# Expert stage of a routed feed-forward layer: which engine reads the expert weights from where

## The reference, cut to what matters

```python
x = x + xattn(layernorm(x), ctx, ctx, mask, ...)
# feed-forward, on layernorm(x); E = 8 experts, D = 128, F = 512
gates = max(softmax(xt @ Wr + br)); idx = argmax(...)
xn = layernorm(xt) * ln_g + ln_b
h = relu(xn @ W1[idx] + b1[idx])        # W1[e] is 128 x 512
y = h @ W2[idx] + b2[idx]               # W2[e] is 512 x 128
x = x + y * gates
```

## Time and profile before

| what | value |
|---|---|
| median of three runs | 397.69 us |
| the profiled execution | 394.74 us |
| its span on the core | 393.0 us |
| VectorE busy | 304.9 us (78%) |
| TensorE matmul busy | 303.1 us (77%) |
| ScalarE busy | 202.0 us (51%) |
| expert stage, first `xh` to last `ot` | 285.7 to 384.7 us |

### The profile page before, as it was taken

How to read it: one execution, slowest core, us unless ns; L and a number is a source line. 1 busy time by engine, 2 the same in 40 slices (tenths; PEclk the granted TensorE clock), 3 DMA queues, 4 the chain that set the end, 5 groups by cost and what they waited for, 6 DMA issues and landing times.

```text
span 393.0 us, 10023 instructions
## 1 busy us (share of the span) xinstructions
PE 303.1 (77%) x3066; PEld 240.2 (61%) x3066; DVE 304.9 (78%) x1159; ACT 202.0 (51%) x548; POOL 163.5 (42%) x220
## 2 busy tenths in 40 slices
PE   0449888788998878877798988963079898978990
PEld 0327656556875655654585776762078887867880
DVE  1247899999989999999999999756747776767771
ACT  1127666466456555646546465511056666656650
POOL 3314445455435545545544543333104443434442
PEclk9999989978568997999968595555569999999997
DMA  5955543234325333424324324000011112112110
GB/s 127 416 132 145 147 137 104 84 111 136 87 85 155 93 90 107 136 84 139 110 85 133 89 84 125 10 14 14 16 42 43 54 54 61 42 50 64 54 32 3
DMA packets 58228, 36.31 MB, mean 92 GB/s; under 512 B 5295, under 2 KB 56116, under 8 KB 58176
## 3 DMA queue, kind: packets, MB, share of 16 engines
q1 hardware_dynamic: 54592, 31.30, 27.5%
q0 software_dynamic: 2272, 4.27, 3.3%
q10 hardware_dynamic: 1312, 0.11, 0.5%
HBM read 14.03 MB, written 22.09 MB: 92 GB/s over the span
## 4 chain that ended last, share of the span: by engine, by line
issue 37%; DVE 31%; POOL 15%; DMA 6%; PE 5%; DVEq 2%; ACTq 1%; POOLq 1%; SPq 0%; ACT 0%
POOL rows_dram L355 5%; DVE Pr L539 3%; DVE mx L535 3%; POOL rs L333 3%; POOL row L343 3%; DMA out<-ot,G 3%; DVE hT L660 3%; DVE xt L500 3%; DVE xh L648 3%; DVE ot L669 2%; POOL xb L338 2%; POOL Kb L348 2%; DMA G<-rows_dram 2%; DVE yb L667 2%; DMA Wr<-in_wr 1%
## 5 line engine op out<-in xcount | busy, mean ns | idle before, releaser
L366 POOL DMA_INDIRECT out<-ot,G x39 | 39.8, 1020 | 67.8 <-DVE ot L669 66.7
L343 POOL TENSOR_TENSOR row<-ve,half 128x2 f32<-128x2 f32 x32 | 24.7, 771 | 103.1 <-DVE ve L589 103.1
L413 ACT ACTIVATE Pr<-Pr,rowany 128x1024 f32<-128x1024 f32 x32 | 36.7, 1148 | 59.8 <-DVE Pr L539 59.8
L706 PE MATMUL ps<-ident,Pr 128*128 128x128 f32 x256 | 51.2, 335 | 0.1
L396 ACT ACTIVATE PT<-ps 128x512 f32<-128x512 f32 x64 | 38.2, 597 | 18.4 <-PE ps L706 17.6
L706 PEld LDWEIGHTS ps<-ident,Pr 128*128 128x128 f32 x256 | 37.0, 173 | 16.8 <-issue 9.1
L796 PE MATMUL ps<-xg,WR 128*128 128x128 f32 x312 | 45.5, 291 | 0.0
L752 PE MATMUL ps<-VB,PT 128*64 128x18 f32 x1024 | 42.1, 228 | 0.3 <-ACT GT L403 0.3
L535 DVE TENSOR_REDUCE mx<-ps 128x16 f32<-128x1024 f32 x32 | 38.9, 1216 | 3.3 <-PE ps L695 3.3
L807 PE MATMUL ps<-WR,hT 128*128 128x128 f32 x312 | 41.2, 276 | 0.0
L796 PEld LDWEIGHTS ps<-xg,WR 128*128 128x128 f32 x312 | 39.5, 199 | 1.4
(11 more groups left out here) (113 smaller groups left out, 633.8 us busy)
## 6 DMA issues: line engine op xcount, KB each, us to landing
rows_dram<-empty SPq DMA_DIRECT2D x32, 528.0 KB, 4.4
WA<-in_wpk SPq DMA_DIRECT2D x8, 578.0 KB, 9.2
G<-rows_dram SPq DMA_DIRECT2D x39, 66.0 KB, 1.9
X<-in_x SPq DMA_DIRECT2D x32, 64.0 KB, 4.1
C<-in_ctxT SPq DMA_DIRECT2D x32, 64.0 KB, 1.8
Cv<-in_ctxT SPq DMA_DIRECT2D x32, 64.0 KB, 2.0
out<-ot,G POOLq DMA_INDIRECT x39, 2.3
rows_dram<-row,posi POOLq DMA_INDIRECT x32, 2.5
```

The lines of the kernel that those rows point to most:

```text
L366: g.indirect_dma_start(out=out, out_offset=bass.IndirectOffsetOnAxis(ap=G[:, q, D + 2:D + 3].bitcast(I32), axis=0), in_=ot[:, q, :], in_of ...
L413: a.activation(Pr[:, q, :], Pr[:, q, :], ACT.Exp, scale=rowany[:, 0:1]).then_inc(s_p, 1)
L706: last = nc.tensor.transpose(ps[:, 4 + m, 128 * j:128 * j + 128], Pr[:, q, 128 * (4 * m + j):128 * (4 * m + j) + 128], ident[:])
```

## The change

The tile `WA` is laid out in another order per expert: W1, b1, b2 and then W2. The ring `WR` holds only W1, b1 and b2 (644 values a partition instead of 1156). ScalarE copies all three of them in one instruction, and VectorE copies nothing. TensorE loads the slot's expert number from `slot` into a register and reads W2 in the down projection straight from `WA` at an address made from it. As the ring buffer now also holds the biases, ScalarE's copy waits for two more readers of the old contents.

```diff
-WP = F + FC * D + FC + D
+WS = F + FC + D
+WP = WS + FC * D
...
-        WR = sb("WR", [P, NW, WP])
+        WR = sb("WR", [P, NW, WS])
...
-        def w2_of(s, c):
-            return WR[:, s % NW, F + D * c:F + D * c + D]
+        def w2_of(ex, c):
+            return WA[:, bass.ds(ex, 1), WS + D * c:WS + D * c + D].rearrange("p e d -> p (e d)")
...
 # ScalarE, stage_w1(s)
                 ex = act.value_load(slot[0:1, 0, s:s + 1], min_val=0, max_val=E - 1)
                 wait(act, b_up, s - NW + 1)
-                a.activation(WR[:, s % NW:s % NW + 1, 0:F], WA[:, bass.ds(ex, 1), 0:F], ACT.Copy).then_inc(b_w1, 1)
+                wait(act, b_rd, (FC - NA) * (s - NW + 1))
+                wait(act, b_y, s - NW + 1)
+                a.activation(WR[:, s % NW:s % NW + 1, :], WA[:, bass.ds(ex, 1), 0:WS], ACT.Copy).then_inc(b_w1, 1)
...
                     act.wait_ge(b_up, s + 1)
-                    act.wait_ge(b_w2, s + 1)
+                    act.wait_ge(b_w1, s + 1)
                     wait(act, b_dn, s - 1)
...
 # VectorE
-            dve.wait_ge(s_we, 128)
-
-            def stage_w2(s):
-                ex = dve.value_load(slot[0:1, 0, s:s + 1], min_val=0, max_val=E - 1)
-                wait(dve, b_dn, s - NW + 1)
-                wait(dve, b_ra, NA * (s - NW + 1))
-                v.tensor_copy(WR[:, s % NW:s % NW + 1, F:WP], WA[:, bass.ds(ex, 1), F:WP]).then_inc(b_w2, 1)
-
-            stage_w2(0)
-            stage_w2(1)
...
                 if s < SLOTS:
+                    dve.wait_ge(b_w1, s + 1)
                     dve.wait_ge(b_up, s + 1)
...
-                if s + 2 < SLOTS:
-                    stage_w2(s + 2)
...
 # TensorE
+            pe.wait_ge(s_we, 128)
...
                     t = s - 1
+                    ex = pe.value_load(slot[0:1, 0, t:t + 1], min_val=0, max_val=E - 1)
                     wait(pe, b_y, t - 1)
-                    pe.wait_ge(b_w2, t + 1)
                     for c in range(FC):
...
                         last = mm(ps[:, 6 + t % 2, 0:D], hT[:, t % 2, P * c:P * c + P], w2_of(ex, c),
```

More of the change, by code:

```diff
@@ L197, in build @@
         w_in = [sem(f"expert_in{u}") for u in range(NW)]
-        b_xh, b_w1, b_w2 = sem("b_normed"), sem("b_w1_staged"), sem("b_w2_staged")
+        b_xh, b_w1 = sem("b_normed"), sem("b_w1_staged")
         g_in = [sem(f"rows_in{u}") for u in range(R)]
@@ L214, in w1_of @@
             return WR[:, s % NW, P * c:P * c + P]
-        def w2_of(s, c):
-            return WR[:, s % NW, F + D * c:F + D * c + D]
+        def w2_of(ex, c):
+            return WA[:, bass.ds(ex, 1), WS + D * c:WS + D * c + D].rearrange("p e d -> p (e d)")
         def b1_of(s, c):
-            return WR[:, s % NW, F + FC * D + c:F + FC * D + c + 1]
+            return WR[:, s % NW, F + c:F + c + 1]
         def b2_of(s):
-            return WR[:, s % NW, F + FC * D + FC:WP]
+            return WR[:, s % NW, F + FC:WS]
         def h_ps(s, c):
@@ L806, in _ @@
                             pe.wait_ge(b_rd, (FC - NA) * t + c - NA + 1)
-                        last = mm(ps[:, 6 + t % 2, 0:D], hT[:, t % 2, P * c:P * c + P], w2_of(t, c),
+                        last = mm(ps[:, 6 + t % 2, 0:D], hT[:, t % 2, P * c:P * c + P], w2_of(ex, c),
                                   start=(c == 0), stop=(c == FC - 1))
@@ L829 @@
             a[f + "W1"],
-            a[f + "W2"].reshape(E, FC, P, D).transpose(0, 2, 1, 3).reshape(E, P, F),
             a[f + "b1"].reshape(E, FC, P).transpose(0, 2, 1),
-            np.broadcast_to(a[f + "b2"][:, None, :], (E, P, D))], axis=2),
+            np.broadcast_to(a[f + "b2"][:, None, :], (E, P, D)),
+            a[f + "W2"].reshape(E, FC, P, D).transpose(0, 2, 1, 3).reshape(E, P, F)], axis=2),
     }
```

## The result

The changed kernel takes 414.13 us (median of four runs, 412.33 to 416.08) against 398.81 us before (four runs, 395.61 to 402.26). The ratio is 1.041 with a 95% interval of 1.031 to 1.051, so it is slower. The profiled execution took 412.74 us with a span of 411.0 us.

What follows compares the result with a forecast made beforehand. VectorE bound the kernel before; a ring through every engine would bound the changed one: 35 turns of 2.76 us against 2.335, 0.5 us of disturbances left, +11.5 us on 397.69, so 409.2 us; range 402 to 420.

Steps and rivals of the forecast that it cites:

- The ring's own range: Expert stage: copy waits for `yb`, relu for copy, down projection for relu, next `yb` for that; 404 to 413 us, chance 70%.
- dear register matmuls: Rival in TensorE's down projection: each matmul pays for its register address, turn up to 3.3 us, 429 us, half 419; chance 10%.
- a falling clock: Rival: TensorE rests about 0.8 us a turn and its clock drops; 440 us if it lasts, a third of it 420; chance 8%.
- The copy's length: ScalarE's copy grows from 512 to 644 values, adding 0.11 us: 0.63 becomes 0.74 us.
- Copy to relu: On ScalarE, copy start to relu start: 0.54 us before, 0.65 us with the longer copy.
- The ring's length: Sum of the pieces of one expert-stage turn through all engines: 2.76 us, against 2.335 before.
- `yb` to copy: VectorE's `yb` start to ScalarE's copy start: 0.32 us until the semaphore is seen, 0.09 for address and start.
- Relu's start to the end of the down projection: ScalarE's relu to TensorE's last down matmul, 1.66 us; chunks 1 to 3 follow both relus, chunk 0 fits in during the second.
- Down projection to `yb`: End of TensorE's last down matmul to start of VectorE's `yb`: 0.04 us.
- The disturbances: Expert-stage turns where `xh` waits for the rows of `G`: 4.3 us in all before, 0.5 us left after.
- TensorE's register: Expert number load on TensorE, about 0.5 us with arithmetic, covered; address before the down projection 0.07 us, once a turn.
- The rival "faster": Expert stage at TensorE's own turn of 1.95 us, held near 2.1 by the reload of `G`; about -8 us, 390; chance 5%.

Runs made afterwards that it cites:

- e1: Changed kernel with ScalarE's two relu chunks of slot s moved ahead of the copy for slot s+2; 393.6 us, ratio 1.000 to the kernel before.
- e2: Changed kernel with four weight ring buffers instead of three, order unchanged; 392.2 us, ratio 0.994 to the kernel before.
- e3: Changed kernel with `yb` adding b2 of expert 0 from `WA`, so the copy does not wait for b_y; 392.7 us, ratio 0.996 to the kernel before.
- e7: Changed kernel with the same waits, the latest semaphore written first at three places; 406.7 us, ratio 1.031 to the kernel before.
- e6: Changed kernel with ten row buffers instead of six, still three weight buffers; 414.7 us, ratio 1.051 to the kernel before.
- e4: Kernel before, all copies kept, but TensorE loads the expert number and reads W2 from `WA` at the register's address; 392.6 us, ratio 0.994.
- e8: Changed kernel without TensorE's register, W2 of expert 0 at a fixed address for all slots; 411.1 us, ratio 1.045 to the kernel before.
- e5: Changed kernel with four weight buffers instead of three and ten row buffers instead of six; 375.8 us, ratio 0.955 to the kernel before.
- e9: Kernel before with ten row buffers for rows and results; 392.8 us, ratio 0.988.

## Why the prediction was right, and where its size was off

The direction, the mechanism and the place were right: VectorE lost its copy and nothing was won, and the wait for b_y closed a ring of one slot a turn (e1, e2 and e3 each open it at a different link). Measured are 414.1 us against 409.2 forecast, +15.3 us against +11.5; the range of 402 to 420 holds it. The ring's own range of 404 to 413 does not: it is missed by 1 us, and what holds the measurement is the part that I had added for the two slow rivals, dear register matmuls and a falling clock, neither of which came.

**The copy's length** was right: 0.74 us forecast and measured. **Copy to relu** too: 319.21 - 318.56 = 0.65 us.

**The ring's length** is the term that was mis-sized, 2.76 us forecast and 3.01 measured. The chain of waits of the changed kernel shows the pieces:

```profile
318.07 0.30 DVE yb L662
318.38 0.02 issue
318.40 0.04 ACTq L51
318.43 0.04 issue
318.47 0.05 ACTq L443
318.52 0.05 issue
318.56 0.06 ACT WR L443
...
319.46 0.37 ACT hT L459
319.83 1.16 PE ps L801 x8
320.99 0.03 issue
321.02 0.02 DVEq L661
321.04 0.04 issue
321.08 0.30 DVE yb L662
```

- `yb` to copy: 318.56 - 318.07 = 0.49 us, where I had 0.41. The row ACTq L51 is a wait instruction of its own (line 51 is the helper that writes waits), 0.04 and 0.04 until the next, in front of the one that forms the address. I had counted only the latter.
- Relu's start to the end of the down projection: 320.99 - 319.21 = 1.78 us against 1.66. I had chunk 1 as the one that decides. In fact chunk 0 did: a wait instruction (L798, 0.051 us each, 37 of them; e7 has none there) and then the address stand before it, and from there all eight loads follow each other without a gap.
- Down projection to `yb`: 0.09 us against 0.04, with the wait instruction DVEq L661.

That is 0.08 + 0.12 + 0.05 = 0.25 us a turn. e7 takes it away without removing a wait, and gets 2.78. So the cause is that of several semaphores, one is waited for by the working instruction (or by the one that forms its address) and the others by instructions of their own ahead of it. In these kernels it is the one written first that rides along: with b_dn written second there are 33 wait instructions on its line, with b_dn written first, in e7, there are none. When the late one is among the others, its own instruction and what stands behind it come only then. Over 35 turns it is 8.8 us; with the 11.5 forecast that makes 20.3, and the expert stage became 20.0 us longer.

**The disturbances** in the ring: 0.5 us forecast. Past the start none of the changed kernel's turns up to slot 36 is over 3.01 us, so there were none. The one turn of 3.22 us at the start comes back in e6 with ten row buffers, so it is not the reload of `G`; its cause stays open. The view of waits still shows `xh` waiting for `G` in three turns, 2.5 us, without effect on the ring.

**TensorE's register.** Forecast: the load is hidden, address 0.07 us in the ring. The load is hidden: e4 has no measurable cost, and in the turn shown it starts at 320.6 us, while the down projection before runs until 320.99. The address costs 0.14 in the ring (e8) and nothing when TensorE is the bound (e5). The rule that the Trainium skill gives in "TensorE: Matmul & The Clock Gate", section "Wait — 56ns, not 53.3ns?", of about 62 ns per matmul in microcode, gave my estimate of 0.124 us from load to load, with the price paid for the weight load and for the matmul. e5 has 0.111 us, as before, so that is not paid here. A price that fits into the 0.111 us would not show.

**The clock** did not fall: 1.00 in the window from 300 to 340 us, and in those up to 400, with the weight loads busy for 26.6 of 40 us. The section "HAM oscillation — how this bites in real kernels" of the same page of the Trainium skill ties a fall to long idle gaps. The expert stage agrees: the gap before each down projection was 1.04 us, and the clock stayed full. The fall in the attention stage, in a window in which TensorE was busy for 4.86 of 5 us, is not explained by it and stays open.

**The rival "faster"** was right in one point that I had only as a side remark. With the ring open, the reload of `G` holds the kernel at about the old time (e1 to e3), at a mean turn of 2.35 to 2.38 us rather than the 2.1 that I had put there. The pace of TensorE came out at 1.90 us (1.95 forecast). With the reload's bound gone, it is reached.

The medians differ by 15.3 us, and the profiled pair by 18.0. The kernel before spreads over up to 8.7 us between executions of one set (390.82 to 399.55). Two profiles of kernels with its turn (e4, e9) had 87.8 and 87.3 us from first to last `yb` where the first one had 90.9; that one has two turns of 3.7 and 4.0 us, which neither of them has. I have not shown that this explains the difference. But the 398.81 us is the highest of the kernel's four medians, and e6, with the changed kernel's turns, lies 19.9 us above the kernel before of its own set (414.68 against 394.81). So the ring was 8.8 us longer than my sum, and that the medians miss the forecast of +11.5 by only 3.8 us is in part luck.

## What to carry to other kernels

Before merging two copies into one, look at who reads each part last: the merged copy waits for the latest reader of all of it, and everything behind it in its engine's order waits too. A buffer that is freed by the end of an item and needed before the middle of the next one can close a ring, whose length is a sum over engines and shows in no busy share; one more buffer, or the copy behind the urgent work, opens it. When a bound is removed, price the next one (here the reload of the row buffers) in the same way, and among several waits before one instruction, try writing the late one first.

## What the hardware showed beyond that

Two waits before a VectorE instruction cost about 0.07 us when the late one is written second (2.94 to 3.01 us at slot 6, in e6 at slot 10). With both waits kept and the late one written first, `yb` starts 0.02 us after the last matmul instead of 0.09 (e7). The order of waits at three places was worth 0.23 us a turn (3.01 to 2.78). A register load on TensorE (0.30 us, and 0.15 us of arithmetic behind it) takes place while earlier matmuls are still running: in e5 there is one in every slot, and TensorE is busy for 40.00 of 40 us. Matmuls whose moving operand lies at a register's address follow each other as fast as others, 0.111 us from load to load.
